# An adjacency layer and a mixture of experts on one core: the order of the setup around the first products

## The reference, cut to what matters

```python
def gnn(H, W, A):                       # H = layernorm(x), x is 8 x 2048 x 128, A = adj is 2048 x 2048
    HW = einsum('bnf,fo->bno', H, W)
    S = relu((A + A.T) * 0.5)
    D = sum(S, axis=1)
    d = where(D > 0, where(D > 0, D, 1) ** -0.5, 0)
    L = eye(2048) - d[:, None] * S * d[None, :]
    return relu(einsum('nm,bmo->bno', L, HW))
x = x + gnn(layernorm(x), L0_gnn_W, adj)
x = x + moe(layernorm(x), ...)          # 8 experts of 128 x 128, the two best of each token are weighed
```

## Time and profile before

| | us |
|---|---|
| median of 3 runs | 878.15 (875.48 to 878.35) |
| profiled execution | 877.46 |
| its span, first to last instruction | 875.7 |
| busy TensorE | 839.2 (96%) |
| busy VectorE | 639.1 (73%) |
| busy ScalarE | 476.0 (54%) |
| busy GpSimd | 324.7 (37%) |
| mean granted TensorE clock | 0.996 |

### The profile page before, as it was taken

One profiled execution on the slowest core, in us unless ns is written; L12 is line 12 of the kernel. 1 busy time (PEld: TensorE's weight loads), 2 busy tenths in 40 slices (PEclk: granted clock), 3 DMA queues, 4 the chain that ended last, 5 costly groups with the idle time before them and its releaser, 6 DMA issues.

```text
span 875.7 us, 14324 instructions
## 1 busy us (share of the span) xinstructions
PE 839.2 (96%) x4098; PEld 697.3 (80%) x4098; DVE 639.1 (73%) x1553; ACT 476.0 (54%) x871; POOL 324.7 (37%) x318
## 2 busy tenths in 40 slices
PE   3687999999999999999999999999999999999998
PEld 3676788888888888888888777788888888888886
DVE  3678645479889644443515599999999999999997
ACT  2686523224333201021110488888888888888886
POOL 1893163474757545555445539101000000000000
PEclk9999999999999999999999999999999999999999
DMA  9991576686866257977778876778767777778772
GB/s 277 325 311 53 220 284 253 240 277 237 272 221 202 85 181 285 334 273 263 255 280 315 303 249 230 267 281 294 289 272 265 257 274 277 273 290 292 286 266 82
DMA packets 93472, 223.00 MB, mean 255 GB/s; under 512 B 8904, under 2 KB 60128, under 8 KB 81520
## 3 DMA queue, kind: packets, MB, share of 16 engines
q1 hardware_dynamic: 88304, 213.23, 68.7%
q0 software_dynamic: 2608, 8.33, 2.4%
q10 hardware_dynamic: 2512, 0.86, 0.4%
HBM read 157.89 MB, written 64.49 MB: 254 GB/s over the span
## 4 chain that ended last, share of the span: by engine, by line
PE 90%; DVE 4%; ACT 2%; DMA 2%; issue 1%; DVEq 0%; ACTq 0%; SPq 0%
PE bank L989 13%; PE bank L991 13%; PE bank L990 13%; PE bank L1489 6%; PE bank L1473 6%; PE bank L1475 6%; PE bank L1486 6%; PE bank L1474 6%; PE bank L1487 6%; PE bank L344 3%; PE bank L936 2%; PE bank L1495 2%; PE bank L474 1%; PE bank L325 1%; DMA b_sb<-in_L_ffn_b 1%
## 5 line engine op out<-in xcount | busy, mean ns | idle before, releaser
L1531 ACT ACTIVATE act_h<-bank,b_sb 128x512 f32<-128x512 f32 x256 | 176.3, 689 | 46.8 <-PE bank L1475 42.5
L1573 DVE TENSOR_TENSOR gated<-c_all,act_h 128x512 f32<-128x512 f32 x256 | 177.4, 693 | 25.5 <-ACT act_h L1531 20.4
L1578 DVE TENSOR_TENSOR g_lo<-gated,g_hi 128x512 fp32r<-128x512 f32 x256 | 175.1, 684 | 0.2
L1538 ACT ACTIVATE g_hi<-gated 128x512 fp32r<-128x512 f32 x256 | 159.5, 623 | 6.1 <-DVE gated L1573 6.1
L1449 POOL DMA_DIRECT2D out<-fin x31 | 23.6, 762 | 308.6 <-DVE fin L1586 308.6
L1105 POOL TENSOR_SCALAR z<-x,mv,rstd 128x128 f32<-128x128 f32 x128 | 106.9, 848 | 3.4
L989 PE MATMUL bank<-y_hi,stage 128*128 128x512 f32 x256 | 105.4, 412 | 2.8 <-issue 1.6
L1051 ACT ACTIVATE z_hl<-bank 128x512 fp32r<-128x512 f32 x32 | 19.1, 597 | 156.4 <-PE bank L936 156.4
L1473 PE MATMUL bank<-z_e,w_hi 128*128 128x512 f32 x256 | 102.8, 402 | 0.1
L1489 PE MATMUL bank<-g_lo,w_hi 128*128 128x512 f32 x256 | 100.9, 394 | 1.1 <-DVE g_lo L1578 1.1
L989 PE MATMUL bank<-y,stage 128*128 128x512 f32 x256 | 101.2, 395 | 0.0
(11 more groups left out here) (133 smaller groups left out, 1487.4 us busy)
## 6 DMA issues: line engine op xcount, KB each, us to landing
c_all<-c_scratch SPq DMA_DIRECT2D x64, 1024.0 KB, 8.1
s_scratch<-stage SPq DMA_DIRECT2D x14, 2048.0 KB, 8.2
stage<-s_scratch SPq DMA_DIRECT2D x14, 2048.0 KB, 8.0
z_e<-z_scratch SPq DMA_DIRECT2D x32, 512.0 KB, 7.3
z_scratch<-z_hl SPq DMA_DIRECT2D x31, 512.0 KB, 2.7
x_raw<-in_x SPq DMA_DIRECT2D x32, 256.0 KB, 6.7
x_res<-in_x SPq DMA_DIRECT2D x32, 256.0 KB, 7.0
r_e<-res_scratch SPq DMA_DIRECT2D x32, 256.0 KB, 2.7
```

The costliest lines, as they stand in the source:

```text
L1531: act.activation(v.act_h[e % R][:, :], ps_h[e % 2][:, :], ACT.Gelu, bias=v.b1_sb[:, e:e + 1]).then_inc(gelu_done, 1)
L1538: act.activation(v.g_hi[e % R][:, :], v.gated[e % R][:, :], ACT.Copy).then_inc(hi_done, 1)
L1573: dve.tensor_tensor(out=v.gated[e % R][:, :], in0=v.c_all[s][:, e, :], in1=v.act_h[e % R][:, :], op=ALU.mult).then_inc(gated_done, 1)
L1578: dve.tensor_tensor(out=v.g_lo[e % R][:, :], in0=v.gated[e % R][:, :], in1=v.g_hi[e % R][:, :].bitcast(FP32), op=ALU.subtract).then_inc(lo ...
```

## The change

GpSimd adds the rows down to j = 9 into `col_sum` (down to 6 before), VectorE adds j = 8, 7 and 6 (5 to 1 before), and rows 5 to 1 are no longer added up: the column sum of k < 5 is a chain of ones-products, one for `col_sum` and one for each block (j, k) with k < j < 6, so 15 ones-products more. The column sums of k = 15 to 12 are made after row 6, those of 11 to 8 after row 10, and those of 7 to 0 inside part 1, after m = 10; before, one was made in each row and the last five after part 0.

The rows loop of every engine ends after row 11, in which the last unit of x is turned. TensorE turns row 12 before the products, and rows 13, 14 and 15 inside part 0, behind the products of m = 14, 13 and 12. VectorE adds rows 13, 14 and 15 between `y_low(14)` and `y_low(11)`, each ahead of the `y_low` of the next block; ScalarE applies the relu of rows 12 to 15 behind all of `y_high(15)` to `y_high(8)` and the direct part and two groups of unit 1. The groups (0, 0) and (0, 1) are turned and split in rows 8 to 10 instead of at the end. `degrees(0)` and the two diagonals stand after the adds of row 10 instead of row 9, and `root(0)` stands on GpSimd ahead of the `invert` of rows 10 and 11. `statistics` stands ahead of the adds in every row. The first three turned groups have their PSUM banks as 2, 2, 2 instead of 2, 3, 2, and both halves of the degrees use bank 7.

```diff
-    FIRST = [(0, None), (0, 0), (0, 1), (1, None), (1, 0), (1, 1), (0, 2), (0, 3), (1, 2), (1, 3)]
+    FIRST = [(0, 0), (0, 1), (0, None), (1, None), (1, 0), (1, 1), (0, 2), (0, 3), (1, 2), (1, 3)]
...
+    def ps_t(G):
+
+        return both_t[0] if G == 1 else both_t[G % 2]
+
+    def turned_before(G):
+
+        return 0 if G == 1 else 1 if G == 2 else G - 2
...
     def turn_group(pe, u, g):
-        if G >= 2:
-            pe.wait_ge(lo_made, ops_with(*part_turned[G - 2]))
+        if G == 3:
+            pe.wait_ge(v.pr.hw_kept, MB - 1)
+        elif G:
+            pe.wait_ge(lo_made, ops_with(*part_turned[turned_before(G)]))
...
-    LAST = 6
-    PARTS_AT = {14: ((0, 1),), 8: ((1, None), (1, 0), (1, 1)), 7: ((0, 2),), 5: ((0, 3),), 3: ((1, 2),), 1: ((1, 3),)}
-    RELU_AT = {13: 2, 12: 1, 11: 0}
-    ADD_AT = {13: 4, 11: 3, 10: 2, 9: 1}
+    LAST = 9
+    ADDED = 6
+    ROWS_APART = 12
...
     def gpsimd(pool):
-        for r, j in enumerate(ROWS):
+        for r, j in enumerate(ROWS[:ROWS_APART]):
...
             if LAST <= j <= MB - 2:
                 add_columns(j)
-            if r == 10:
+            if r == 9:
                 root(0)
         root(1)
...
     def scalar(act):
-        for r, j in enumerate(ROWS):
+        for r, j in enumerate(ROWS[:ROWS_APART]):
             for k in jobs(r):
                 pr.copy_x(act, k)
             for g in range(n_groups(j)):
                 relu(r, j, g)
             for k in jobs(r):
                 if k:
                     pr.keep(act, k - 1)
+            if r in (8, 10):
+                st.high_group(act, 0, r // 2 - 4)
+        st.high_direct(act, 0)
+        for m in range(15, 7, -1):
+            y_high(m)
+        st.high_direct(act, 1)
+        st.high_group(act, 1, 0)
+        st.high_group(act, 1, 1)
+        for r in range(ROWS_APART, MB):
+            relu(r, MB - 1 - r, 0)
+        pr.keep(act, MB - 1)
         act.wait_ge(pr.xt_turned, MB)
         act.wait_ge(pr.x_mv_done, MB)
+        st.high_group(act, 0, 2)
+        for m in range(7, -1, -1):
             y_high(m)
...
     def column_sum(k):
-            pe.matmul(ps_d[part_of(k)][:, k:k + 1], column, v.one_col[:, :], start=True, stop=True).then_inc(col_done, 1)
+            rest = range(k + 1, ADDED)
+            if rest:
+                pe.wait_ge(relued, until_row(k + 1))
+            last = pe.matmul(ps_d[part_of(k)][:, k:k + 1], column, v.one_col[:, :], start=True, stop=not rest)
+            for j in rest:
+                last = pe.matmul(ps_d[part_of(k)][:, k:k + 1], s_tri[:, block(j, k), :], v.one_col[:, :], start=False,
+                                 stop=(j == ADDED - 1))
+            last.then_inc(col_done, 1)
...
     def tensor(pe):
-            if j + 2 < MB and r < 13:
-                column_sum(j + 2)
-            if r == 13:
-                pr.project(pe, MB - 1)
-        pe.wait_ge(deg_step, 2)
-        pe.wait_ge(pr.hw_kept, MB - 1)
-        for g in range(2):
-            st.turn_group(pe, 0, g)
+            if r == 6:
+                for k in (15, 14, 13, 12):
+                    column_sum(k)
+            if r == 8:
+                pe.wait_ge(relued, until_row(MB - 1))
+                st.turn_group(pe, 0, 0)
+            if r == 10:
+                for k in (11, 10, 9, 8):
+                    column_sum(k)
+                st.turn_group(pe, 0, 1)
+        pr.project(pe, MB - 1)
+        turn(12, 3, 0)
...
     def vector(dve):
+        for r, j in enumerate(ROWS[:ROWS_APART]):
+            for k in jobs(r):
+                pr.statistics(dve, k)
             for g in range(n_groups(j)):
                 add(r, j, g)
             if r == 9:
+                st.low_group(dve, 0, 0)
+            if r == 10:
                 degrees(0)
                 for u in range(2):
                     st.diagonal(dve, u)
+                st.low_group(dve, 0, 1)
         st.low_direct(dve, 0)
+        add_columns(8)
+        add(12, 3, 0)
+        y_low(15)
+        y_low(14)
+        add(13, 2, 0)
+        y_low(13)
+        add(14, 1, 0)
+        y_low(12)
+        add(15, 0, 0)
+        for m in range(11, 7, -1):
             y_low(m)
+        st.low_direct(dve, 1)
+        st.low_group(dve, 1, 0)
+        st.low_group(dve, 1, 1)
+        add_columns(7)
+        add_columns(6)
+        degrees(1)
+        st.low_group(dve, 0, 2)
+        for m in range(7, -1, -1):
+            y_low(m)
+            if m == 5:
+                st.low_group(dve, 0, 3)
             if m == 3:
+                st.low_group(dve, 1, 2)
+            if m == 1:
+                st.low_group(dve, 1, 3)
                 outward()
...
-        turns = [{12: ((1, 0), (1, 1))}, {14: ((0, 2),), 11: ((0, 3),)}, {6: ((1, 2),), 3: ((1, 3),)},
+        turns = [{11: ((1, 0),), 10: ((1, 1),)}, {12: ((0, 2),), 9: ((0, 3),)}, {5: ((1, 2),), 3: ((1, 3),)},
                  {5: ((2, 0), (2, 1)), 2: ((2, 2), (2, 3))}]
+        row_at = {14: 13, 13: 14, 12: 15}
...
                 products(u, m, u, acc[u], MB - 1 - m)
                 for unit_of, g in turns[part].get(m, ()):
                     st.turn_group(pe, unit_of, g)
-            if part == 0:
-                for k in range(4, -1, -1):
-                    v.column_sum(k)
+                if part == 0 and m in row_at:
+                    v.turn_last(row_at[m], MB - 1 - row_at[m], 0)
+                if part == 1 and m == 10:
+                    for k in range(7, -1, -1):
+                        v.column_sum(k)
```

More of the change, by code:

```diff
@@ L469, in turn_group @@
         a, b = blocks(u, g)
-        if G >= 2:
-            pe.wait_ge(lo_made, ops_with(*part_turned[G - 2]))
+        if G == 3:
+            pe.wait_ge(v.pr.hw_kept, MB - 1)
+        elif G:
+            pe.wait_ge(lo_made, ops_with(*part_turned[turned_before(G)]))
         for m in range(a, b):
             i = m - a
-            last = pe.transpose(ps_t[G % 2][:, i * P:(i + 1) * P], v.s_tri[:, block(n, m), :], v.ident[:, :])
+            last = pe.transpose(ps_t(G)[:, i * P:(i + 1) * P], v.s_tri[:, block(n, m), :], v.ident[:, :])
         last.then_inc(s_turned, 1)
@@ L480, in high_group @@
         act.wait_ge(s_turned, G + 1)
-        act.activation(v.stage[u % 2][:, 0, a:b, :].rearrange("p m f -> p (m f)"), ps_t[G % 2][:, 0:(b - a) * P],
+        act.activation(v.stage[u % 2][:, 0, a:b, :].rearrange("p m f -> p (m f)"), ps_t(G)[:, 0:(b - a) * P],
                        ACT.Copy).then_inc(hi_made, 1)
@@ L542, in setup_stage @@
     v.acc_free = 34
-    ps_d = [v.banks[2], v.banks[7]]
+    ps_d = [v.banks[7], v.banks[7]]
     def n_groups(j):
@@ L657, in scalar @@
                     pr.keep(act, k - 1)
+            if r in (8, 10):
[9 more added lines that the diff above has]
+        pr.keep(act, MB - 1)
         act.wait_ge(pr.xt_turned, MB)
         act.wait_ge(pr.x_mv_done, MB)
-        st.high_direct(act, 0)
-        st.high_group(act, 0, 0)
-        for m in range(MB - 1, -1, -1):
+        st.high_group(act, 0, 2)
+        for m in range(7, -1, -1):
             y_high(m)
-            if m in RELU_AT:
-                relu(MB - 1 - RELU_AT[m], RELU_AT[m], 0)
-            if m == 7:
-                pr.keep(act, MB - 1)
-            for u, g in PARTS_AT.get(m, ()):
-                if g is None:
-                    st.high_direct(act, u)
-                else:
-                    st.high_group(act, u, g)
+            if m == 5:
+                st.high_group(act, 0, 3)
+            if m == 3:
+                st.high_group(act, 1, 2)
+            if m == 1:
+                st.high_group(act, 1, 3)
     def tensor(pe):
@@ L701, in column_sum @@
                 column = v.col_sum[:, k, :]
-                wait(pe, col_added, min(14 - k, 14))
-            pe.matmul(ps_d[part_of(k)][:, k:k + 1], column, v.one_col[:, :], start=True, stop=True).then_inc(col_done, 1)
+                wait(pe, col_added, min(14 - k, 15 - ADDED))
+            rest = range(k + 1, ADDED)
[6 more added lines that the diff above has]
+            last.then_inc(col_done, 1)
         pe.wait_ge(small_in, 16 * v.small_loads)
         pr.average_w(pe)
-        for r, j in enumerate(ROWS):
+        for r, j in enumerate(ROWS[:ROWS_APART]):
             for k in jobs(r):
@@ L713, in tensor @@
                 turn(r, j, g)
[L714 to L722 removed]
+            if r == 6:
[10 more added lines that the diff above has]
+        turn(12, 3, 0)
+        v.column_sum, v.turn_last = column_sum, turn
     def vector(dve):
@@ L771, in vector @@
         pr.centre_w(dve)
-        for r, j in enumerate(ROWS):
-            if r < 9:
-                for k in jobs(r):
-                    pr.statistics(dve, k)
+        for r, j in enumerate(ROWS[:ROWS_APART]):
+            for k in jobs(r):
+                pr.statistics(dve, k)
             for g in range(n_groups(j)):
                 add(r, j, g)
-            if r >= 9:
-                for k in jobs(r):
-                    pr.statistics(dve, k)
             if r == 9:
```

(27 more changed lines are left out.)

7 lines of the change are left out of this document (2 added, 5 removed).

## The result

The changed kernel takes 893.02 us, median of 6 runs (890.62 to 896.05), beside 878.40 for the kernel before (6 runs, 875.48 to 880.07): a ratio of 1.017, 95% interval 1.0144 to 1.0197, or 14.6 us slower. Its profiled execution took 894.74 us with a span of 893.1, against 877.46 and 875.7. The direction is as forecast. The size is not: +9.0 was forecast, and +17.4 of span came in the profiled pair. The profiled execution was the second slowest of its six: their mean granted TensorE clocks go from 0.982 (896.05 us) and 0.983 (894.74, the profiled one) over 0.988 (892.51) to 0.990 (890.62). So part of what the profile shows of the clock is this execution's own.

A forecast was written before the change was run, and what follows sets the result against it. TensorE was taken as the bound, so whatever the setup delays or adds behind about 80 us moves the end. The terms -1.2 + 2.85 + 3.7 + 2.1 + 0.1 + 1.5 gave +9.0 on 877.46: 886.5 us, range 881 to 891.

The forecast's parts named there:

- start of products: Up to the first product on TensorE: it begins at 77.4 instead of 78.62, -1.2 us.
- ring in part 0, at full clock: Unit 0, m = 15 to 8: products, turn, add and y_low wait on each other for three blocks, +2.85 us.
- column sums, without clock: Inside part 1: 46 ones-product instructions at 0.103 us, 4.74 us instead of 1.03, +3.7 us.
- wait for the lower half: Ahead of part 2: TensorE waits for the chain from last column sum to y_low, no longer hidden, +2.1 us.
- part 2, without clock: Part 2 runs at VectorE's pace, 7.5 instead of 7.37 us, +0.1 us.
- clock: In part 0: first two blocks' products and row 13's turn at 1.2 GHz, +1.5 us, bounds 0 and 3.
- Rival B: Second low clock ahead of part 2 and part 0's rounds at 1.2 GHz: +11.5 to +14 us, chance 0.10.
- Rival A: Same mechanisms, small sizes: clock holds, sums and part 0's rounds go faster; +4 to +6.5 us, chance 0.22.
- C: Products fill TensorE's holes, beginning before 75.5 and never waiting again: -2.7 us, 874.8, chance 0.06.
- D: Nothing to measure over the whole kernel, within 0.3% (2.6 us): 877.5 us, chance 0.06.

The follow-up runs named there:

- a_fill: The changed kernel with unread transposes filling TensorE's holes ahead of and in part 0 and ahead of part 2: 889.47 us, ratio 1.0148.
- b_ones: The kernel before with rows 5 to 1 not added up by VectorE and 15 more ones-products behind part 0 instead: 883.54 us, ratio 1.0063.
- b_diag: The kernel before with the two diagonals moved on VectorE behind the adds of row 11: 876.93 us, ratio 0.9986.
- a_noring: The changed kernel with rows 13 to 15 turned and added behind row 12, ahead of the products: 886.40 us, ratio 1.0111.
- b_narrow: The kernel before with 15 needless ones-products (30 one-column instructions) behind the column sums after part 0: 885.69 us, ratio 1.0084.
- a_rows_added: The changed kernel with rows 5 to 1 added up by VectorE again, so 16 column sum instructions instead of 46: 888.39 us, ratio 1.0136.
- a_noring_added: The changed kernel with rows 13 to 15 turned and added ahead of the products and rows 5 to 1 added by VectorE: 882.74 us, ratio 1.0052.
- a_fill_added: The changed kernel with rows 5 to 1 added by VectorE and filling transposes ahead of and in part 0, none ahead of part 2: 885.29 us, ratio 1.0081.
- b_wide: The kernel before with 30 needless transposes of 128 columns behind the column sums after part 0: 884.72 us, ratio 1.0062.

## Why the prediction was right in direction and short in size

| step | forecast | measured | read from |
|---|---|---|---|
| start of products | -1.2 | -0.04 | 78.58; -1.13 counted from row 10 |
| ring in part 0, at full clock | +2.85 | +3.70 | part 0 of a_fill 11.30, less 7.60 |
| column sums, without clock | +3.7 | +3.99 | 46 at 0.109, less 1.03 |
| wait for the lower half | +2.1 | +2.24 | the rest of part 1: 14.33 less 5.59, less 6.50 |
| part 2, without clock | +0.1 | +0.27 | 0.99 less 0.72 |
| clock | +1.5 | +6.50 | 5.21 + 0.57 + 0.72 |
| up to unit 2 | +9.05 | +16.66 | |

**The step that failed is the clock**, with 5.0 of the 7.6 us. It was put at 1.5, as the first two blocks' products and one turn at 1.2 GHz, with 3 as its upper bound, after the low stretch of before. That stretch was read as the microsecond from 73 to 74; it lasted 3.4 us, which the rows beside the new profile's show, and the walk put no price on a clock that stays down while products come with waits between them. That "the clock held through other holes of 2 us" is true in the trace of before for the holes of 2.12 us up to 13.94 and 2.43 up to 43.96, but behind the one of 2.08 up to 28.06 the clock is at 0.50 from 30 to 32.

Measured were three terms. In part 0 it is 5.21 (16.51 less 11.30 with the holes filled): the first six products went 0.43 us apart, for 0.23 at full clock, about as taken, but the ring's turns and all products up to 93 did so too. At the end of the ones-products it is 0.57 (the last ten took 1.66 us, 103.58 to 105.24, for 1.09 at the price of the first 36). At the start of part 2 it is 0.72 (the first three products 1.41 us, 109.42 to 110.83, for 0.69).

Rival B named both places, the ring rounds and a second low clock near part 2, but its +11.5 to +14 ends below the median's +14.6, and it had the second fall come of the hole of 2.1 us. The chance given to it, 0.10, leaned on the sentence that TensorE is dense ahead of that hole. Dense it was, and the clock fell nevertheless, within that dense stretch. These 6.50 us are the profiled execution's. From the mean clocks, an estimate: at 0.983 it was low for 30 us in all ((1 - 0.983) / 0.5 of 893), at the 0.988 of the median runs for 21, so the median holds less of the clock. The profile of before had no long run of ones-products from which the second fall could be read; the bound should have been taken over all of the new order's work up to unit 2, not over the first few products.

**The start** was right by its mechanism. VectorE stood at `low_direct(0)` for 2.11 us (forecast 2.1), the root began at 69.17 and the first product came 11.95 us after row 10 instead of 13.08. That row 10 landed 1.09 later in this profile ate it, which the medians, over other runs, need not share: it is 1.1 of the 2.7 us between the profiled pair's +17.3 and the medians' +14.6. The rule of the Trainium skill, "GPSIMD Engine Reference", section "Key points", that GpSimd contends with VectorE instructions with two SBUF inputs, fits the 1901 ns of the longest diagonal of the earlier trace rows, beside the add. For the root the kernel after bears out the prediction, which expected no hold, and not the rule, by which the second diagonal was to end with the root: the two, 69.33 to 69.94, ran beside the root, 69.17 to 70.81, and took 0.61 us together.

**The ring** waits 1.31, 1.18 and 1.04, forecast 1.25, 1.1 and 1.0. As these waits were taken at full clock for turns and products, and measured at half, their agreement says that the chain of turn, add and `y_low` between two blocks was read rightly, and is in part luck; with the holes filled TensorE still waits 0.44, 0.30 and 0.17 for `y_lo` behind eight fillers. Its full-clock price is 0.85 over the forecast. The fillers can't be it, since TensorE waited behind them each time. Most of it lies in the three rounds, which take 6.97 us in that trace (76.53 to 83.50) for 6.3 in the walk (`y_low(14)` at 78.0 to `y_low(11)` at 84.3): 0.24 of it in three products behind a wait, which take 0.81 us (79.02 to 79.83, 81.38 to 82.19) for the 0.69 of the walk, and the rest, by difference, in the handovers between the engines.

**The sums** are 46 instructions at 0.109 us, and 0.103 was taken. The floor of about 25 ns in the Trainium skill, "TensorE: Matmul & The Clock Gate", section "Wait — 56ns, not 53.3ns?", would have given 1.2 us for all, an estimate; the trace has 5.59, so it does not price one-column fp32 products here. That the adds on VectorE which they replace "gave nothing back" was too strong: b_ones shows up to 1.4 us for them (0.7 in the start, 0.6 in part 0).

**The wait for the lower half** is confirmed by itself in three traces (2.10 us each time). In the kernel after it shows as only 0.42, since the products ahead of it run at 1.2 GHz and fill it, and a reader of that row alone would call the term wrong.

Rival A (the clock holds), C (products fill the holes) and D (no change) are out: the products began at 78.58, where C needed 75.5, and waited three times in part 0. What the runs leave open is why the clock falls and when it comes back: they show where it was low and what that cost, and nothing of its cause.

## What to carry over

An order that puts single waits of 1 us between a few products costs more than these waits: look at the granted clock of the stretch, and price all of its work at both levels of the clock, not only the first few products. Where matmul work is added to spare another engine, ask how far that engine was on the path: VectorE's adds of rows 5 to 1 mostly stood beside busy TensorE and gave back 1.4 us at most, while their replacement cost 4 to 4.7 us and the clock behind it. Before costing an early start, walk every engine's queue up to it, since the gain usually ends at the next instruction that waits in order; and compare from a common event (here row 10's turn), not from the start of the span.

## What was not expected of the hardware

**TensorE's clock fell while TensorE was busy all the time.** In five traces the granted clock went to 0.50 within a run of 40 to 46 instructions of one column: after (104.1 to 110.9), a_fill (95 to 102), a_noring (from 95.6), b_ones (from 87.7) and b_narrow (89.8 to 96.6). Behind 10 or 16 of them it held (before, a_rows_added, a_noring_added, a_fill_added), and behind 30 transposes of 128 columns too in the one trace of b_wide. Each kernel has one trace, nothing between these cases was run, and b_wide's other runs leave open whether the column count matters. So these are cases and no rule.

**A VectorE instruction can be held for as long as one of GpSimd's lasts**, and whether it is depends on the pair. Held were a diagonal, 1901 ns for 343, beside GpSimd's add of 768 columns, and an aggregate step of a single input, started 0.44 us late beside the same add. Beside GpSimd's root (1.64 us) an add of 640 columns took 0.83, in line with its size, and two diagonals took 0.61 in the kernel after and 0.60 in b_diag.
